# Swapped q and k rows by VectorE's shuffle instead of a second projection, with thirteen tasks of the mix bank laid anew

## The chip, the cores and the metric

One NeuronCore of one Trainium2 chip runs the whole program. The metric is device time in microseconds (us) of one execution; three executions of the kernel before have a median of 373.65 us. Its engines are TensorE (PE: matmuls; PEld: its weight loads), VectorE (DVE), ScalarE (ACT), GpSimd (POOL) and SyncE (SP), each working through its own instructions in order and waiting for the others on semaphores.

## What is computed

A transformer block on 2 x 1024 tokens of width 128, in fp32: attention with 16 heads of width 8, layer norm, a gated feed-forward part with four hidden tiles of 128, layer norm. Of the attention, the part that the change touches is the norm of q and k and the rotation of each half of a head by the other:

```python
half = D // 2
def rot(x):
    x1, x2 = (x[..., :half], x[..., half:])
    return jnp.concatenate([-x2, x1], axis=-1)
...
q, k = _rmsnorm(q, q_scale), _rmsnorm(k, k_scale)     # mean of squares over the 8 of a head
q, k = q * cos + rot(q) * sin, k * cos + rot(k) * sin
...
attn = jax.nn.softmax(q @ k.T, axis=-1)                # after q is scaled by HEAD_DIM ** -0.5
out = (attn @ v) @ w_proj + b_proj
```

## The kernel before

**Layout.** q and k are held transposed: a partition is a feature (8 in a row belong to one head), the free axis holds tokens. The tokens go in four chunks of 512. A chunk of queries is handled in 32 steps: 4 groups of 4 heads, and for each group 8 tiles of 128 keys. A step on TensorE is two pairs of logits (L508, each pair 128 keys by 2 heads by 512 queries into one of three two-bank PSUM tiles) and then the values of the step before (L522, four matmuls of 9 columns each, one a head, which are added up over 8 steps in the O bank, bank 6). ScalarE takes the exponential of each pair (L886, 128x1024), 64 in a chunk, numbered u = 0 to 63. The logits of a pair can be written only when the exponential that last used the PSUM tile has ended, three pairs before.

**The turn of a group.** After 8 steps VectorE moves the O bank to SBUF and turns it (turn_o, L1052), divides by the sums (L1058, L1060), and signals o_copied. The values of the first step of the next group overwrite the O bank, so TensorE waits there (in `values`: if kt == 0, for o_copied) with everything queued behind, the logits that ScalarE takes next among it.

**The mix bank.** Bank 7 serves all that is not attention proper, one task at a time, in a fixed order; each task's TensorE part waits until the one before is read out (mix_free). In the first chunk these tasks prepare q and k of the later token tiles. There are five such blocks (LATE, n = 0 to 4: q of tile 1, k and q of tiles 2 and 3). In the kernel before a block takes three tasks: "proj" (one 128x512 matmul by the weights), "swap" (the same by weights whose columns are swapped within each head, QS or KS of wq) and "var" (the squares by a matrix of means). Two tasks project v of tiles 2 and 3 here ("v"; one more, of tile 1, comes first), and a last one ("flag") tells whether the ternary weights' low parts are all zero. TASK_SLOTS says at which half step TensorE issues each: slot 2s stands between the logits and the values of step s, slot 2s + 1 behind those values. SQUARE_PAIRS and RINV_PAIRS say behind which exponential ScalarE does a block's square (L870, from PSUM) and its Ln and Exp (L877, L879: 1 over the root of the mean).

**VectorE in the first chunk** runs a hand-written list (first_chunk, from L1229): late_products (bank by cosine, waits for the square), late_swap (bank by sine), late_sum, late_rows (by the inverse root, L1202, then the two parts for the store, L1002 and L1004), the turns, and beside these the splits of the weights in a high and a low part (split_weights, L1219 and L1220), the addition of the bias to x (L1247) and four reductions for the flag (largest_low, L1223), whose result (L1274, w_split) the "flag" task takes. VectorE then writes the flags, and TensorE and the others read them (lo_flag) before the loop over chunks 1 to 3 begins. ScalarE loads another table between (L907). GpSimd issues the stores of the parts and the weight loads; SyncE fetches each group's rows.

Of the kernel before, what the change touches and what calls it, by code (L numbers as in the profile page):

```python
# [34 lines left out]
LOGIT_BOUND = 60.0  # L35


MIX_FIRST = 19
MIX_CHUNK = 20

CHAIN_CHUNK = 29
# [39 lines left out]
TASKS = (("v", 1), ("proj", 0), ("swap", 0), ("var", 0),  # L81
         ("proj", 1), ("swap", 1), ("var", 1),
         ("proj", 2), ("swap", 2), ("var", 2), ("v", 2),
         ("proj", 3), ("swap", 3), ("var", 3),
         ("proj", 4), ("swap", 4), ("var", 4), ("v", 3), ("flag", 0))
TASK_SLOTS = (5, 10, 18, 22, 23, 26, 30, 31, 34, 38, 40, 42, 46, 48, 50, 54, 56, 59, 62)
V_PAIR = 7
SQUARE_PAIRS = (11, 23, 31, 43, 51)
RINV_PAIRS = (22, 30, 38, 49, 57)


def tiles_in_turn(swaps):
# [27 lines left out]
def build(nc, x_t, x_n, w_qkv, cols, scale_rows, bias, w_proj, w1, w2, h1, h2, w3, tables, means, eye, out):  # L120
    ctx = ExitStack()
    with ctx:
# [347 lines left out]
        def _(pe):  # L470
# [130 lines left out]
            def first_task(n):  # L601

                kind, i = TASKS[n]
                bank = mix(0)
                if n == 0:
                    pe.wait_ge(rot_done, 8)
                if kind == "flag":
                    pe.wait_ge(w_split, 1)
                    mm = pe.matmul(bank[0:1, 0:1], ve[:, 0:1], ones_c[:], start=True, stop=True)
                elif kind == "v":  # L610
                    mm = project_v(bank, i)
                elif kind == "var":
                    pe.wait_ge(late_sq, i + 1)
                    mm = variance(bank, late_sets[i % 2][0])
                else:
                    t, of = LATE[i]
                    pe.wait_ge(in_x[t], 16)
                    mm = proj(of + (QS if kind == "swap" else 0), bank, t)
                mm.then_inc(mix_ready, 1)

            def keep_warm(count, bank=MIX_BANK):
# [194 lines left out]
        def _(act):  # L816
# [47 lines left out]
                act.nop().then_inc(mix_free, 1)  # L864

            def late_square(n):
                act.wait_ge(mix_ready, TASKS.index(("proj", n)) + 1)
                if n >= 2:
                    act.wait_ge(parts_done, PARTS * (n + 2))
                nc.scalar.activation(late_sets[n % 2][0], ps[:, MIX_BANK, :], ACT.Square).then_inc(late_sq, 1)  # L870

            def late_inverse_root(n):

# [65 lines left out]
        def _(dve):  # L939
# [289 lines left out]
            def first_chunk():  # L1229
# [15 lines left out]
                late_products(1)
                dve.wait_ge(in_res, 64)
                link(nc.vector.tensor_tensor(xb[:], xb[:], bias_b[:, None, :].to_broadcast([P, NCH * TILES, P]), ALU.add), 0)  # L1247
                late_swap(1)
                late_sum(0)
                late_rows(0)  # L1250
# [3 lines left out]
                late_swap(2)
                late_sum(1)
                late_rows(1)
                dve.wait_ge(h1_taken, 1)
                largest_low(0, H1, HM * HID)
# [16 lines left out]
                late_rows(3)
                late_sum(4)
                late_rows(4)
                late_v(3)
# [173 lines left out]
```

## Time and profile before

| | |
|---|---|
| three executions | 373.52, 373.65, 376.35 us (median 373.65) |
| profiled execution, its own time | 374.06 us |
| its span, first to last instruction | 372.0 us |
| mean granted TensorE clock | 0.986 of 2.4 GHz |
| TensorE, ScalarE, VectorE busy | 92%, 82%, 60% of the span |

The span leaves 2.06 us of the profiled execution outside it. Times in rows are microseconds from the span's start unless marked ns. A timeline row joins neighbouring instructions of one line: it gives the start, the length of the whole and the number joined; idle time in front of it and what ended that stand in brackets. TensorE's records count two passes for each fp32 matmul, so one step's values are x8, a projection x2. Busy TensorE is not TensorE at its peak, since matmul ends are modelled and overlap. Waits named for a releaser are inferred.

### The profile page before, as it was taken

The page shows a single profiled execution, that of the slowest core. Times are in us where ns is not written, and L with a number is a line of the kernel's source. Part 1 is how long each engine was busy: PE and PEld are TensorE (multiplying, and loading weights), DVE is VectorE, ACT ScalarE, POOL GpSimd, SP SyncE. Part 2 cuts the span into 40 slices and gives each one's busy share as a digit, 9 for nine tenths or more (in the row PEclk, how much of TensorE's full clock was granted, in tenths as well). Part 3 has the DMA queues.
Part 4 walks back from the last instruction along what each step waited for, and adds up shares of the span by engine and source line. Part 5 has one row for each costly group of instructions (what it writes and reads, how often), then busy time and mean ns, then how long its engine had stood idle before and what let it go on. Part 6 is the DMA issues. An engine that isn't in the chain of part 4 may idle for free.

```text
span 372.0 us, 6282 instructions
## 1 busy us (share of the span) xinstructions
PE 341.7 (92%) x2096; PEld 137.3 (37%) x2101; DVE 221.8 (60%) x468; ACT 305.7 (82%) x353; POOL 29.8 (8%) x43
## 2 busy tenths in 40 slices
PE   8898999998999989999999899999999899999980
PEld 4422223222332444443232544433224544435850
DVE  3996988775457625464467363545576253667753
ACT  3689999899999889789999897989998897854330
POOL 3032111103100000001100000011000000011001
PEclk9989999999999999999999999999999999999996
DMA  7829545326212110201110200203021100000001
GB/s 217 299 104 320 170 160 182 146 90 237 94 34 76 48 56 2 71 32 68 60 65 36 92 9 10 90 0 102 30 97 36 64 0 0 0 29 2 0 0 33
DMA packets 12741, 29.42 MB, mean 79 GB/s; under 512 B 1056, under 2 KB 5040, under 8 KB 12720
## 3 DMA queue, kind: packets, MB, share of 16 engines
q1 hardware_dynamic: 8896, 16.75, 13.3%
q0 software_dynamic: 3392, 12.07, 9.1%
q10 hardware_dynamic: 432, 0.33, 0.4%
q8 instruction: 12, 0.20, 0.3%
q14 instruction: 9, 0.07, 0.1%
HBM read 17.64 MB, written 9.44 MB: 73 GB/s over the span
## 4 chain that ended last, share of the span: by engine, by line
PE 68%; ACT 12%; DVE 10%; issue 6%; DMA 1%; POOL 1%; POOLq 0%; ACTq 0%; DVEq 0%
PE ps L522 25%; PE ps L569 15%; PE ps L508 13%; ACT probs L886 10%; PE ps L688 4%; PE ps L559 4%; DVE ffn L1115 2%; PE ps L472 2%; PE ps L623 2%; DMA srow<-in_scale_rows 1%; PE ps L722 1%; PE ps L539 1%; DVE ffn L1112 1%; PE ps L484 1%; DVE ffn L1129 1%
## 5 line engine op out<-in xcount | busy, mean ns | idle before, releaser
L886 ACT ACTIVATE probs<-ps 128x1024 f32<-128x1024 f32 x256 | 242.8, 1035 | 24.8 <-PE ps L508 24.1
L522 PE MATMUL ps<-probs,va 128*9 128x512 f32 x896 | 112.6, 594 | 3.7 <-ACT probs L886 2.8
L508 PE MATMUL ps<-qa,ka 32*128 32x512 f32 x512 | 77.7, 497 | 6.6 <-ACT probs L886 5.6
L508 PEld LDWEIGHTS ps<-qa,ka 32*128 32x128 f32 x512 | 31.9, 183 | 104.1 <-ACT probs L886 57.4
L1115 DVE TENSOR_SCALAR ffn<-ps,col 128x512 f32<-128x512 f32 x36 | 27.0, 751 | 55.0 <-PE ps L569 50.9
L569 PE MATMUL ps<-g_hi,w_hi 128*128 128x512 f32 x108 | 45.5, 421 | 1.6 <-DVE ffn L1115 1.2
L569 PE MATMUL ps<-g_lo,w_hi 128*128 128x512 f32 x108 | 42.4, 393 | 0.0
L522 PEld LDWEIGHTS ps<-probs,va 128*9 128x9 f32 x896 | 15.8, 89 | 48.9 <-issue 27.6
L1090 DVE TENSOR_TENSOR g_lo<-ffn,g_hi 128x512 fp32r<-128x512 f32 x36 | 24.9, 692 | 1.2
L569 PEld LDWEIGHTS ps<-g_hi,w_hi 128*128 128x128 f32 x108 | 20.2, 187 | 14.5 <-DVE g_lo L1090 4.0
L450 POOL TENSOR_TENSOR rs<-ve,mhalf 128x4 f32<-128x4 f32 x6 | 6.1, 1022 | 228.1 <-DVE ve L1078 228.1
L569 PEld LDWEIGHTS ps<-g_lo,w_hi 128*128 128x128 f32 x108 | 20.3, 188 | 3.4
L522 PE MATMUL ps<-probs,v_all 128*9 128x512 f32 x128 | 17.0, 602 | 1.2 <-ACT probs L886 1.2
L1089 DVE CAST g_hi<-ffn 128x512 fp32r<-128x512 f32 x36 | 15.2, 423 | 4.5 <-ACT ffn L897 3.4
L1052 DVE STREAM_TRANSPOSE o_tok<-ps 128x512 f32<-128x512 f32 x15 | 10.7, 715 | 12.0 <-PE ps L522 12.0
L1112 DVE SCALAR_TENSOR_TENSOR ffn<-ps,col,ffn 128x512 f32<-128x512 f32 x12 | 9.0, 751 | 11.7 <-PE ps L559 11.7
L472 PE MATMUL ps<-xT,wq 128*128 128x512 f32 x28 | 15.1, 633 | 0.1
L897 ACT ACTIVATE ffn<-ffn 128x512 f32<-128x512 f32 (+1 forms) x18 | 12.9, 765 | 2.1 <-DVEq L1119 2.1
L559 PE MATMUL ps<-x_hi,w_hi 128*128 128x512 f32 x24 | 11.9, 496 | 2.9 <-DVE ffn L1115 2.2
L969 DVE SCALAR_TENSOR_TENSOR ffn<-ps,col,rope 128x512 f32<-128x512 f32 x13 | 9.7, 749 | 6.7 <-ACT ffn L870 3.7
L623 PE MATMUL ps<-warm 128*128 128x512 bf16 x48 | 12.8, 393 | 1.0 <-issue 1.0
L930 ACT ACTIVATE ffn<-ps,col 128x512 f32<-128x512 f32 x8 | 4.8, 689 | 9.4 <-PE ps L688 9.4
(133 smaller groups left out, 329.1 us busy)
## 6 DMA issues: line engine op xcount, KB each, us to landing
ka<-k_scr SPq DMA_DIRECT2D x14, 512.0 KB
k_scr<-parts POOLq DMA_DIRECT2D x8, 512.0 KB, 4.2
q_scr<-parts POOLq DMA_DIRECT2D x8, 512.0 KB, 4.8
qa<-q_scr SPq DMA_DIRECT2D x14, 256.0 KB
va<-v_all SPq DMA_DIRECT2D x14, 144.0 KB
ffn<-in_h POOLq DMA_DIRECT2D x1, 1024.0 KB, 9.1
h_raw<-in_h POOLq DMA_DIRECT2D x1, 1024.0 KB, 7.2
xT<-in_x_t SPq DMA_DIRECT2D x3, 256.0 KB, 6.1
```

The lines of the kernel that those rows point to most:

```text
L472: return pe.matmul(bank, wq[:, W_AT[i]:W_AT[i] + P], xT[:, t * CH:(t + 1) * CH], start=True, stop=True)
L508: mm = pe.matmul(s_tile(u)[:, i, :], ka[rows, slot, kt * P:(kt + 1) * P], qa[rows, slot, :], start=True, stop=not shifted)
L522: mm = pe.matmul(ps[32 * h:32 * h + VW, O_BANK, :], v, probs[:, step % 4, h, :], start=(kt == 0), stop=(kt == KT - 1))
L559: mm = pe.matmul(bank, a, x, start=(j == 0), stop=(j == len(todo) - 1))
L569: mm = pe.matmul(bank, w, x, start=(k == 0 and i == 0), stop=(k == HM - 1 and i == len(todo) - 1))
L623: pe.matmul(ps[:, bank, :], warm[:, 0:P], warm[:], start=True, stop=True)
L688: mm = pe.matmul(ps[:, bank0 + m, :], a, (g_hi, g_lo)[part][:, k, :], start=(k == 0 and part == 0 and i == 0), stop=(k == HM - 1 and part ...
L886: nc.scalar.activation(probs[:, step % 4, 2 * pair:2 * pair + 2, :], s_tile(u), ACT.Exp).then_inc(exp_done, 1)
L897: nc.scalar.activation(act_o[:, cols], pre_a[:, cols], ACT.Gelu).then_inc(act_done, 1)
L1089: link(nc.vector.tensor_copy(hi, src), cb)
L1090: return nc.vector.tensor_tensor(lo, src, hi.bitcast(F32), ALU.subtract)
L1115: ins = nc.vector.tensor_scalar(a, mix_bank, col[:, c0 + m:c0 + m + 1], None, ALU.mult)
```

## The change

- The five "swap" tasks go, and with them five projections by the swapped weights. The mix bank has 14 tasks in the first chunk instead of 19.
- In their place late_products first copies the bank to SBUF with the rows of each head turned by half (stream_shuffle on VectorE, by the list HALF_TURN), signals that copy (late_raw), and then multiplies the bank by the cosine. Both no longer wait for a square.
- ScalarE squares the shuffled copy in SBUF instead of the bank. The order of a head's eight rows is another, their sum is the same.
- late_turn takes the place of late_swap: it waits for the square, and multiplies the shuffled copy by the sine, in place.
- The slots of all tasks but the first and the last are new, and so are the places of ScalarE's squares and roots. VectorE's list is in another order.

```diff
-TASK_SLOTS = (5, 10, 18, 22, 23, 26, 30, 31, 34, 38, 40, 42, 46, 48, 50, 54, 56, 59, 62)
+TASK_SLOTS = (5, 12, 18, 21, 26, 30, 34, 36, 39, 44, 47, 52, 56, 62)
...
-SQUARE_PAIRS = (11, 23, 31, 43, 51)
-RINV_PAIRS = (22, 30, 38, 49, 57)
+SQUARE_PAIRS = (15, 23, 32, 41, 49)
+RINV_PAIRS = (19, 27, 35, 45, 53)
+HALF_TURN = [m // HD * HD + (m + HD // 2) % HD for m in range(32)]
...
             def late_square(n):
-                act.wait_ge(mix_ready, TASKS.index(("proj", n)) + 1)
-                if n >= 2:
-                    act.wait_ge(parts_done, PARTS * (n + 2))
-                nc.scalar.activation(late_sets[n % 2][0], ps[:, MIX_BANK, :], ACT.Square).then_inc(late_sq, 1)
+                act.wait_ge(late_raw, n + 1)
+                nc.scalar.activation(late_sets[n % 2][0], late_sets[n % 2][2], ACT.Square).then_inc(late_sq, 1)
...
             def late_products(n):
-                h = late_sets[n % 2][1]
-                mixed(0)
+                h, rot = late_sets[n % 2][1:]
+                k = mixed(0)
+                use[0] += 1
+                t, of = LATE[n]
+                nc.vector.stream_shuffle(rot, mix_bank, HALF_TURN).then_inc(late_raw, 1)
+                turned_by(mix_bank, of, t, h).then_inc(mix_free, 1)
+                dve.wait_ge(mix_free, k + 1)
+
+            def late_turn(n):
+
+                rot = late_sets[n % 2][2]
                 t, of = LATE[n]
                 dve.wait_ge(late_sq, n + 1)
-                turned_by(mix_bank, of, t, h).then_inc(mix_free, 1)
-
-            def late_swap(n):
-
-                t, of = LATE[n]
-                k = mixed(0)
-                use[0] += 1
-                turned_by(mix_bank, of + QS, t, late_sets[n % 2][2]).then_inc(mix_free, 1)
-                dve.wait_ge(mix_free, k + 1)
+                link(turned_by(rot, of + QS, t, rot), 0)
```

The order on each engine is shown at three places. The line numbers after the change are lower by 1 to 3 up to VectorE's list: L507, L521, L471, L483 are the logits, values, projection and means of before's L508, L522, L472, L484.

First TensorE, from the values of step 13 to those of step 16, the first of group 2, which wait for the second turn. Before (v_all is read for groups 0 and 1, va from group 2 on):

```order
L522 MATMUL ps<-probs,v_all 9x512 x4
L508 MATMUL ps<-qa,ka 128x512 x4
L484 MATMUL ps<-ffn,mean 128x512
L522 MATMUL ps<-probs,v_all 9x512 x4
L472 MATMUL ps<-xT,wq 128x512
L508 MATMUL ps<-qa,ka 128x512 x4
L522 MATMUL ps<-probs,v_all 9x512 x4
L508 MATMUL ps<-qa,ka 128x512 x4
L472 MATMUL ps<-xT,wq 128x512
L522 MATMUL ps<-probs,va 9x512 x4
```

After, the same stretch:

```order
L521 MATMUL ps<-probs,v_all 9x512 x4
L507 MATMUL ps<-qa,ka 128x512 x4
L471 MATMUL ps<-xT,wq 128x512
L521 MATMUL ps<-probs,v_all 9x512 x4
L507 MATMUL ps<-qa,ka 128x512 x4
L521 MATMUL ps<-probs,v_all 9x512 x4
L507 MATMUL ps<-qa,ka 128x512 x4
L483 MATMUL ps<-ffn,mean 128x512
L521 MATMUL ps<-probs,va 9x512 x4
```

Before, three tasks lie in this stretch (block 1's means, block 2's projection and swap), and the swap is the last ahead of the values of step 16. After, there are two: block 2's projection, a slot earlier than it was, and block 2's means, which now stand last. Block 1's means lie further ahead (slot 26, where it was 30).

Then VectorE around the same turn (L1052 before, L1049 after). Before:

```order
L1219 CAST w_hi<-h_raw 128x1024
L1220 TENSOR_TENSOR w_lo<-h_raw,w_hi 128x1024
L969 SCALAR_TENSOR_TENSOR ffn<-ps,col,rope 128x512
L1052 STREAM_TRANSPOSE o_tok<-ps 128x512
L1058 RECIPROCAL rden<-o_tok 128x16
L1060 TENSOR_TENSOR attn<-o_tok,rden 128x16x8
L969 SCALAR_TENSOR_TENSOR ffn<-ps,col,rope 128x512
L1195 TENSOR_TENSOR ffn<-ffn 128x512
L1202 TENSOR_TENSOR ffn<-ffn 128x512
L1002 CAST parts<-ffn 128x512
L1004 TENSOR_TENSOR parts<-ffn,parts 128x512
```

After:

```order
L1179 STREAM_SHUFFLE ffn<-ps 128x512
L966 SCALAR_TENSOR_TENSOR ffn<-ps,col,rope 128x512
L1200 TENSOR_TENSOR ffn<-ffn 128x512
L999 CAST parts<-ffn 128x512
L1001 TENSOR_TENSOR parts<-ffn,parts 128x512
L1217 CAST w_hi<-h_raw 128x1024
L1218 TENSOR_TENSOR w_lo<-h_raw,w_hi 128x1024
L1049 STREAM_TRANSPOSE o_tok<-ps 128x512
L1055 RECIPROCAL rden<-o_tok 128x16
L1057 TENSOR_TENSOR attn<-o_tok,rden 128x16x8
L966 SCALAR_TENSOR_TENSOR ffn<-ffn,col,rope 128x512
L1193 TENSOR_TENSOR ffn<-ffn 128x512
```

Before, one product stood between the split of the second hidden weight (L1220 on h_raw) and the turn, and that product was block 2's own. Now block 2's shuffle and product come first, then block 1's inverse root and its two parts (L1200, L999, L1001), then the split, and then the turn. The third turn has block 4's shuffle and product and block 3's rows in front of it in the same way.

Last the end of VectorE's list. Before:

```order
L1223 TENSOR_REDUCE stats<-w_lo 128x1 x2
L1274 TENSOR_REDUCE ve<-stats 128x1
L1202 TENSOR_TENSOR ffn<-ffn 128x512
L1002 CAST parts<-ffn 128x512
L1004 TENSOR_TENSOR parts<-ffn,parts 128x512
L1195 TENSOR_TENSOR ffn<-ffn 128x512
L1202 TENSOR_TENSOR ffn<-ffn 128x512
L1002 CAST parts<-ffn 128x512
L1004 TENSOR_TENSOR parts<-ffn,parts 128x512
L1208 COPY v_all<-ps 128x4x4x8 x4
L1280 TENSOR_SCALAR flags<-ps 1x1
```

After:

```order
L1218 TENSOR_TENSOR w_lo<-ffn,w_hi 128x512
L1221 TENSOR_REDUCE stats<-w_lo 128x1
L1200 TENSOR_TENSOR ffn<-ffn 128x512
L999 CAST parts<-ffn 128x512
L1001 TENSOR_TENSOR parts<-ffn,parts 128x512
L1206 COPY v_all<-ps 128x4x4x8 x4
L1221 TENSOR_REDUCE stats<-w_lo 128x1
L1274 TENSOR_TENSOR xb<-xb,bias_b 128x2048
L1221 TENSOR_REDUCE stats<-w_lo 128x1
L1276 TENSOR_REDUCE ve<-stats 128x1
L1278 TENSOR_SCALAR flags<-ps 1x1
L1279 SCALAR_TENSOR_TENSOR flags<-flags 1x1
```

The addition of the bias (xb) came in the middle of the list before and now stands next to the end, between the last reductions. The reduction on which the flag task waits (writes ve) stood before the last two blocks' rows and the copy of v, and is now behind all of them.

## Rows read from the trace of the kernel before

**Rows 1.** The page: busy time, share and instructions of each engine.
```profile
PE 341.7 (92%) x2096; PEld 137.3 (37%) x2101; DVE 221.8 (60%) x468; ACT 305.7 (82%) x353; POOL 29.8 (8%) x43
```

**Rows 2.** Busy time by stretch: the first chunk from pair 8 on.
```profile
core 0: us, PE busy (x) PEld busy (x) DVE busy (x) ACT busy (x) POOL busy (x), PEclk, DMA share, GB/s
27.00:90.10 63.10, 60.02 (x376) 16.48 (x372) 50.12 (x79) 60.54 (x71) 10.99 (x16) 1.00 0.55 190
```

**Rows 3.** Groups by line, 27 to 90.2 us: busy and mean, idle before.
```profile
line engine op names shapes xcount | busy us, mean ns | idle before us <-releasers
L886 ACT ACTIVATE probs<-ps 128x1024 f32<-128x1024 f32 x56 | 53.0, 1042 | 2.5 <-PE ps L508 2.4 <-ACT v_all L836 0.2
...
L969 DVE SCALAR_TENSOR_TENSOR ffn<-ps,col,rope 128x512 f32<-128x512 f32 x10 | 7.5, 751 | 6.7 <-ACT ffn L870 3.7 <-PE ps L472 2.2 <-issue 0.8
...
L877 ACT ACTIVATE ffn<-ps,eps_c 128x512 f32<-128x512 f32 x5 | 3.5, 698 | 0.0
...
L879 ACT ACTIVATE ffn<-ffn 128x512 f32<-128x512 f32 x5 | 3.2, 631 | 0.2
L870 ACT ACTIVATE ffn<-ps 128x512 f32<-128x512 f32 x5 | 3.0, 608 | 0.0
```

**Rows 4.** Timeline, ScalarE: start, length, and in brackets idle before it.
```profile
27.05 3.77 ACT L886 ACTIVATE probs<-ps 128x1024 f32<-128x1024 f32 x4 [0.17 <-ACT v_all L836]
...
39.02 2.85 ACT L886 ACTIVATE probs<-ps 128x1024 f32<-128x1024 f32 x3 [0.37 <-PE ps L508]
...
48.47 2.85 ACT L886 ACTIVATE probs<-ps 128x1024 f32<-128x1024 f32 x3 [0.31 <-PE ps L508]
...
67.82 3.77 ACT L886 ACTIVATE probs<-ps 128x1024 f32<-128x1024 f32 x4 [0.73 <-PE ps L508]
...
90.11 1.28 ACT L907 ACT_TABLE_LOAD   x1
91.41 7.44 ACT L886 ACTIVATE probs<-ps 128x1024 f32<-128x1024 f32 x8
```

**Rows 5.** Timeline, TensorE, where group 2 begins and at the chunk's end.
```profile
55.36 1.12 PE L472 MATMUL ps<-xT,wq 128*128 128x512 f32 x2
56.41 1.05 PE L522 MATMUL ps<-probs,va 128*9 128x512 f32 x8
...
88.32 1.05 PE L522 MATMUL ps<-probs,va 128*9 128x512 f32 x8 [0.17 <-ACT probs L886]
90.61 0.63 PE L508 MATMUL ps<-qa,ka 32*128 32x512 f32 x4 [1.25 <-ACT probs L886]
```

**Rows 6.** Timeline, VectorE: a shuffle, and the work around the second turn.
```profile
27.65 0.72 DVE L992 STREAM_SHUFFLE r<-ffn 128x512 f32<-128x512 f32 x1
...
42.19 0.69 DVE L1219 CAST w_hi<-h_raw 128x1024 fp32r<-128x1024 f32 x1
...
45.27 2.28 DVE L1247 TENSOR_TENSOR xb<-xb,bias_b 128x2048 f32<-128x2048 f32 x1
...
50.90 0.85 DVE L1219 CAST w_hi<-h_raw 128x1024 fp32r<-128x1024 f32 x1
51.78 1.23 DVE L1220 TENSOR_TENSOR w_lo<-h_raw,w_hi 128x1024 fp32r<-128x1024 f32 x1
...
54.76 0.71 DVE L1052 STREAM_TRANSPOSE o_tok<-ps 128x512 f32<-128x512 f32 x1
...
58.10 0.69 DVE L1202 TENSOR_TENSOR ffn<-ffn 128x512 f32<-128x512 f32 x1
58.83 0.43 DVE L1002 CAST parts<-ffn 128x512 fp32r<-128x512 f32 x1
...
80.81 1.81 DVE L1223 TENSOR_REDUCE stats<-w_lo 128x1 f32<-128x1024 f32 x2
...
87.03 0.88 DVE L1208 COPY v_all<-ps 128x128 f32<-128x128 f32 x4
...
88.55 0.14 DVE L1282 CAST flags_i<-flags 1x1 int32<-1x1 f32 x1
```

More of the change, by code:

```diff
@@ L35 @@
 LOGIT_BOUND = 60.0
-MIX_FIRST = 19
+MIX_FIRST = 14
 MIX_CHUNK = 20
@@ L80 @@
 LATE = ((1, Q), (2, K), (2, Q), (3, K), (3, Q))
[L81 to L85, printed above, removed]
-TASK_SLOTS = (5, 10, 18, 22, 23, 26, 30, 31, 34, 38, 40, 42, 46, 48, 50, 54, 56, 59, 62)
+TASKS = (("v", 1), ("proj", 0), ("var", 0), ("proj", 1), ("var", 1), ("proj", 2), ("var", 2), ("v", 2),
+         ("proj", 3), ("var", 3), ("proj", 4), ("var", 4), ("v", 3), ("flag", 0))
+TASK_SLOTS = (5, 12, 18, 21, 26, 30, 34, 36, 39, 44, 47, 52, 56, 62)
 V_PAIR = 7
-SQUARE_PAIRS = (11, 23, 31, 43, 51)
-RINV_PAIRS = (22, 30, 38, 49, 57)
+SQUARE_PAIRS = (15, 23, 32, 41, 49)
+RINV_PAIRS = (19, 27, 35, 45, 53)
+HALF_TURN = [m // HD * HD + (m + HD // 2) % HD for m in range(32)]
 def tiles_in_turn(swaps):
@@ L228, in build @@
         sq_done = sem("sq_done")
+        late_raw = sem("late_half_turned")
         late_sq = sem("late_square_done")
@@ L617, in first_task @@
                     pe.wait_ge(in_x[t], 16)
-                    mm = proj(of + (QS if kind == "swap" else 0), bank, t)
+                    mm = proj(of, bank, t)
                 mm.then_inc(mix_ready, 1)
@@ L1237, in first_chunk @@
                 late_products(0)
-                turn_group(0)
-                late_swap(0)
                 dve.wait_ge(in_h1, 16)
                 split_half(h1_raw, H1, 0)
+                turn_group(0)
+                late_turn(0)
+                late_sum(0)
+                late_products(1)
                 split_half(h1_raw, H1, 1).then_inc(h1_taken, 1)
+                late_rows(0)
+                late_turn(1)
+                late_sum(1)
                 dve.wait_ge(in_h2, 16)
                 split_half(h2_raw, H2, 0)
[L1245 to L1250, printed above, removed]
+                late_products(2)
+                late_rows(1)
                 link(split_half(h2_raw, H2, 1), 0)
-                late_products(2)
                 turn_group(1)
[L1254 to L1258, printed above, removed]
+                late_turn(2)
                 late_sum(2)
@@ L1262, in first_chunk @@
                 late_products(3)
-                largest_low(1, H2, HM * HID)
-                late_swap(3)
+                dve.wait_ge(h1_taken, 1)
+                largest_low(0, H1, HM * HID)
+                late_turn(3)
+                late_sum(3)
                 dve.wait_ge(in_w123, 48)
                 split_weights(w_raw[:, 0:2 * HID], W1, 2 * HID)
+                late_products(4)
+                late_rows(3)
                 turn_group(2)
+                late_turn(4)
+                late_sum(4)
                 link(split_weights(w_raw[:, 2 * HID:2 * HID + HM * P], W3, HM * P), 0)
-                late_products(4)
-                late_sum(3)
-                late_swap(4)
+                largest_low(1, H2, HM * HID)
+                late_rows(4)
+                late_v(3)
                 largest_low(2, W1, 2 * HID)
+                dve.wait_ge(in_res, 64)
+                nc.vector.tensor_tensor(xb[:], xb[:], bias_b[:, None, :].to_broadcast([P, NCH * TILES, P]), ALU.add)
                 link(largest_low(3, W3, HM * P), 0)
                 nc.vector.tensor_reduce(ve[:, 0:1], w_max[:, 0:4], AX.X, ALU.max).then_inc(w_split, 1)
[L1275 to L1278, printed above, removed]
                 mixed(0)
```

## The prediction

> **What bounds the kernel now.** The page's first part comes first: TensorE is busy 92% of the span, ScalarE 82%, VectorE 60% [rows 1]. The change touches only the first chunk, so the next view is the busy time of that stretch alone. From 27.0 us, where pair 8 begins, to 90.1, TensorE has 60.0 and ScalarE 60.5 of 63.1 us at a granted clock of 1.00; VectorE has 50.1 [rows 2]. So two engines are nearly full, and the question is which ends each wait. The groups by line answer: ahead of its 56 exponentials ScalarE idled 2.5 us in all, 2.4 of it for TensorE's logits [rows 3]. The timeline shows these as short pieces, 0.37, 0.31 and 0.73, and three more of 0.31 to 0.32, while between them the exponentials run one behind the other [rows 4]. ScalarE sets the pace of this chunk and TensorE's tasks push it off by 2.35 us. That is also the most that a perfect rearrangement can give, for ScalarE keeps all its work. VectorE's 6.7 us of idle time ahead of its products [rows 3] cost nothing by themselves.
>
> **What goes and what comes.** (a) Five swaps go: 5 x 1.06 = 5.3 us of TensorE (1.12 by the row, of which about 0.06 lies under the next matmul: 55.36 to 56.41) [rows 5]. TensorE is not first in the chain, so this can give back only parts of the 2.35. (b) Five shuffles are added on VectorE. No row has one that reads PSUM. Those that read SBUF take 0.72 us, the transposition of the same 128x512 out of PSUM takes 0.71, a plain cast 0.43, and the four copies of v out of PSUM 0.88 together [rows 6]. I take 0.72 as the nearest in kind, with 0.43 and 0.88 as bounds. (c) The five sine products now read SBUF, and stay at the 0.75 us that these products have on average [rows 3]. (d) ScalarE's square reads SBUF. From PSUM it took 608 ns; an activation of the same size from SBUF, the exponential of L879, 631, and the slowest of that size, L877, 698 [rows 3]. I take 0.02 each, 0.1 in all; nothing and 0.45 are the bounds.
>
> By the Trainium skill, VectorE: DVE Perf Modes, section on the TRN2 errata, a ScalarE instruction has a fixed part of 224 cycles out of SBUF and of 172 out of PSUM; as an estimate from that page this speaks against (d) with 43 ns each, 0.2 us in all. The trace agrees in sign, at 23 ns, and by that rule the forecast would be 0.1 us later.
>
> **The walk.** What is left is order: when does each engine reach its waits? I follow the changed program with the pitches of these rows. An exponential takes 0.92 to 0.93 (8 in 7.44, the last 1.02 long), I use 0.925, and ends 1.02 after its start [rows 4]; Ln with Exp takes 1.27 and a square about 0.48, both their lengths of 0.70, 0.63 and 0.61 less the overlap of some 0.1 with what follows. On TensorE values take 0.98, a step's logits 0.44 when nothing holds them (they are ready 0.5 after the start), a task 1.06, less the same overlap [rows 5]. A VectorE instruction that the next one waits for takes its length and 0.03.
>
> *Pair 14.* Pair 8 starts at 27.05 [rows 4], so ScalarE wants pair 14 at 27.05 + 6 x 0.925 = 32.6; the square that stood behind pair 11 and gave TensorE half a microsecond now comes behind pair 15. TensorE starts the values of step 4 when exponential 9 ends (29.0). Behind them come logits, block 0's projection (slot 12), values and the logits of step 7: 29.0 + 0.98 + 0.44 + 1.06 + 0.98 + 0.5 = 33.0. Idle 0.4.
>
> *Pairs 20 and 28.* No swap stands ahead of them any more; the 0.37 and 0.31 go. Up to pair 28 ScalarE does one Ln and Exp more than before (behind pair 27, not 30), so it starts pair 28 at 48.47 + 1.27 - 0.68 + 0.40 = 49.5.
>
> *Pair 32.* TensorE's second logits of step 15 wait for exponential 28 (50.5), the projection of block 2 follows at 50.9 and is ready at 52.05; values to 53.0, logits ready at 53.5. ScalarE wants them at 49.5 + 4 x 0.925 = 53.2. Idle 0.35.
>
> *The second turn.* VectorE has waited for this projection. From 52.1 it does shuffle 0.75, product 0.78, block 1's inverse root 0.72, cast 0.46, subtraction 0.61 (0.69 less an overlap of 0.08), then the split's cast, 0.72 if it is not stretched, and subtraction, 1.26 [rows 3, 6]. It starts the transposition at 57.4 and ends it at 58.1. Before, it started it at 54.76, right behind one product [rows 6]. TensorE wants the O bank as soon as block 2's means are done. The square behind pair 32 ends at 55.0, the means at 56.1. So the values of step 16 wait 56.1 to 58.1, where before they went without a wait at 56.41 [rows 5]. This stall of 2.0 us is the main step of the forecast. ScalarE has pairs up to 35 and Ln and Exp, until 59.0. TensorE brings pair 36 at 58.1 + 0.98 + 0.53 = 59.6: idle 0.6. Then the v task (slot 36) stands ahead of pair 38 (59.5 + 1.09 + 0.98 + 0.53 = 62.1, wanted at 61.5: 0.6) and block 3's projection (slot 39) with values ahead of pair 40 (64.6, wanted 64.0: 0.6). Sum 1.8.
>
> *The third turn.* Exponential 45 ends at 64.6 + 5 x 0.925 + 0.48 + 1.02 = 70.7, then values to 71.7, block 4's projection to 72.85. VectorE: shuffle, product, block 3's root, cast and subtraction, 3.3 us, so the transposition runs from 76.2 to 76.9. TensorE wants the O bank at 75.3. ScalarE, with its square behind pair 49, wants pair 52 at 77.9, and gets it at 76.95 + 0.98 + 0.53 = 78.5: idle 0.6. The catching up, with the tasks of slots 52 and 56, costs about 0.35 more, an estimate from the 0.31 to 0.37 that single tasks cost before [rows 4].
>
> *Sum.* Idle after: 0.4 + 0.35 + 1.8 + 0.6 + 0.35 = 3.5 us, where it was 2.35. With 0.1 for the squares that is +1.25. The profiled execution took 374.06 us, so 375.3; it lay 0.4 above the median of 373.65, by which it is 374.9. I give **375.0 us**, +1.2 on either within rounding.
>
> *The end of the chunk.* VectorE goes on from 76.9: the rest of the turn 0.6, product and sum 1.5, split 1.1, the reduction of 2048 elements 2.2 (as the bias addition of that length, 2.28 with overlap), root and parts 1.8, then, from 84.2 when v is there, copies 0.95, reductions 1.1 + 0.5, the bias 2.2, the last reduction 0.2 [rows 6]: w_split at 89.2. TensorE is then at the flag task, 89.0. So the bias, which cost nothing in the middle of the list, has almost no cover left here. Flags are written at 90.1. TensorE ends its values at 90.4, needs 1.3 us for load and branch (88.32 + 0.98 to 90.61) and has logits at 92.3 [rows 5]. ScalarE ends at about 91.2 and its table at 92.5 [rows 4]. This just fits, by 0.2 us, as it did before (91.1 to 91.41). I cost it at nothing; every tenth that VectorE loses beyond these 0.2 costs a tenth. The later chunks' code stays and starts later by the same 1.2. GpSimd's three weight loads wait for the first hidden weight's second half, which is now split behind block 1's product, about 2 us later than it was. Behind them GpSimd holds the stores of blocks 0 to 4. Block 0's parts come earlier in VectorE's list than before, and the first use of any of these is the next chunk's, so I cost this at nothing.
>
> **Rivals.**
> *The turns don't bind (faster).* If VectorE ends the second turn by 59.0 - 0.98 - 0.53 = 57.4, 0.7 earlier than walked, pair 36 loses nothing; shuffles at their lower bound (0.3 earlier) with a projection 0.4 earlier would do it. With both turns free there remain 0.4, 0.35, some 0.85 at pairs 38 and 40 where tasks crowd, and 0.4: 2.0 against 2.35, so 0.35 faster, 373.3. If all idle goes too, 371.3 (373.65 - 2.35). For it speaks the 5.3 us taken off TensorE; against it, that in these rows VectorE had one product ahead of the turn and now has seven instructions. Chance 0.25.
> *The end comes late (slower still).* If VectorE is later than walked by 1 us, from a shuffle at 0.88 (0.8 in all) and casts that stretch beside GpSimd's stores, as 0.85 for 0.69 in these rows [rows 6], then the turns and w_split each pass on most of it: 0.3 + 0.3 at the turns and 0.7 at the end, +2.5, so 376.2. Against it: VectorE still idles about 2 us ahead of blocks 2 and 4, which takes up what came before. Chance 0.13.
> *Nothing seen (within 0.4 of before).* The squares are cheap and one turn binds, the other not: 3.5 - 1.0 = 2.5 of idle, 373.8. Chance 0.12.
> My forecast, both turns bind, +0.5 to +2: 0.50.
>
> **Numbers.** The range runs from the free turns to the late end with its bounds: 373.1 to 376.6. It leaves out the case of no idle at all and a late end past 3 us. A measurement of this kernel can tell about 1%, 3.7 us, from no change. The most that can be gained is 2.35, so faster by that much is next to excluded, 0.01; slower by 3.7 needs the late end at 1.5 times its price, 0.04; within 1% has 0.95.
>
> **What would show it.** In the changed profile ScalarE's idle ahead of its exponentials in this chunk should sum to about 3.5 us, with gaps of 0.5 to 0.7 at pairs 36, 38, 40 and 52 (about 59, 62, 64 and 78 us). The values' wait for the transposition should appear as about 2 us twice; the second transposition should start near 57.4. The table load should come near 91.3, where it came at 90.11. Shuffles should read 0.72, squares 0.63. The forecast is wrong if the transpositions start before 56.5, if the table load comes before 90.1, or if more than 0.3 us pass between the table's end and the next exponential.

## The result, and the profile after

The changed kernel takes **378.9 us** (median of 4 runs, 376.3 to 379.9) where the kernel before took 373.7 beside it: ratio 1.0127, 95% interval 1.0095 to 1.0158. It is slower by 5.2 us; that is 3.9 above the forecast of 375.0 and outside its range of 373.1 to 376.6, and a loss of over 3.7 us had been given a chance of 0.04. In this document an execution more than 1.5% above the fastest of its kernel is left out of the ratios, but not of the medians and ranges.

The profiled execution took 379.01 us. ScalarE's timeline, with the idle time ahead of a row in brackets, shows where the time went:

```profile
33.05 1.94 ACT L883 ACTIVATE probs<-ps 128x1024 f32<-128x1024 f32 x2 [0.47 <-PE ps L507]
35.34 0.63 ACT L867 ACTIVATE ffn<-ffn 128x512 f32<-128x512 f32 x1 [0.35 <-DVE ffn L1179]
...
53.99 1.02 ACT L883 ACTIVATE probs<-ps 128x1024 f32<-128x1024 f32 x1 [0.31 <-PE ps L507]
...
61.48 1.94 ACT L883 ACTIVATE probs<-ps 128x1024 f32<-128x1024 f32 x2 [1.96 <-PE ps L507]
65.75 1.94 ACT L883 ACTIVATE probs<-ps 128x1024 f32<-128x1024 f32 x2 [2.34 <-PE ps L507]
68.22 1.02 ACT L883 ACTIVATE probs<-ps 128x1024 f32<-128x1024 f32 x1 [0.52 <-PE ps L507]
...
82.25 1.94 ACT L883 ACTIVATE probs<-ps 128x1024 f32<-128x1024 f32 x2 [0.68 <-PE ps L507]
...
86.36 3.77 ACT L883 ACTIVATE probs<-ps 128x1024 f32<-128x1024 f32 x4 [0.90 <-PE ps L507]
90.48 1.02 ACT L883 ACTIVATE probs<-ps 128x1024 f32<-128x1024 f32 x1 [0.34 <-PE ps L507]
...
96.10 1.28 ACT L904 ACT_TABLE_LOAD   x1
97.39 1.02 ACT L883 ACTIVATE probs<-ps 128x1024 f32<-128x1024 f32 x1
```

The table load comes at 96.10, where it came at 90.11 [rows 4]. From pair 8 to there it is 6.1 us more, so the loss is made in this one chunk. The gaps lie where the walk put them (pairs 14, 32, 36, 38, 40, 52 and the catching up, 0.90 and 0.34), and one more, 0.35, stands ahead of the first square. Those at 36, 38 and the catching up are more than three times their forecast size. The groups by line say the same: 7.7 us of idle ahead of the exponentials against 2.5 [rows 3].

```profile
L883 ACT ACTIVATE probs<-ps 128x1024 f32<-128x1024 f32 x56 | 53.1, 1030 | 7.7 <-PE ps L507 7.5 <-ACT v_all L835 0.2
L1179 DVE STREAM_SHUFFLE ffn<-ps 128x512 f32<-128x512 f32 x5 | 3.7, 737 | 0.0
L867 ACT ACTIVATE ffn<-ffn 128x512 f32<-128x512 f32 x5 | 3.2, 634 | 0.4 <-DVE ffn L1179 0.4
```

What made them large stands in TensorE's timeline around the second and the third turn:

```profile
55.68 1.10 PE L483 MATMUL ps<-ffn,mean 128*128 128x512 f32 x2
58.81 1.90 PE L521 MATMUL ps<-probs,va 128*9 128x512 f32 x8 [2.04 <-DVE o_tok L1049]
...
61.37 2.08 PE L478 MATMUL ps<-wq,xT 128*128 128x128 f32 x8
63.38 1.90 PE L521 MATMUL ps<-probs,va 128*9 128x512 f32 x8
...
80.73 1.04 PE L521 MATMUL ps<-probs,va 128*9 128x512 f32 x8 [1.80 <-ACT probs L883]
...
82.14 1.93 PE L483 MATMUL ps<-ffn,mean 128*128 128x512 f32 x2
84.01 1.88 PE L521 MATMUL ps<-probs,va 128*9 128x512 f32 x8
```

The stall of 2.04 us is the one that was forecast, 0.7 us later. But the values behind it take 1.90 us, not 1.05 [rows 5], and the v task 2.08: TensorE works at half speed until 65.3. Behind the stall of 1.80 (put down to the exponential; VectorE's transposition, from 79.88 to 80.59, ended last) values and logits still take their usual time, and from about 82.3 to 85.7 the same happens. The windows carry the reason in the third column from the end, the granted clock:

```profile
core 0: us, PE busy (x) PEld busy (x) DVE busy (x) ACT busy (x) POOL busy (x), PEclk, DMA share, GB/s
27.00:58.00 31.00, 26.70 (x164) 6.86 (x160) 26.16 (x44) 29.80 (x35) 7.97 (x12) 1.00 0.67 232
58.00:66.00 8.00, 7.19 (x36) 2.67 (x40) 4.89 (x12) 3.66 (x6) 0.00 (x0) 0.57 0.42 160
...
80.00:88.00 8.00, 7.27 (x39) 1.65 (x40) 7.69 (x11) 6.39 (x8) 1.39 (x3) 0.79 0.54 195
```

In single microseconds from 59 to 65 it is 0.50, the lower of the two levels, 1.2 GHz for 2.4. Before, it was 1.00 from pair 8 to the table load [rows 2]. By the Trainium skill, TensorE: Matmul & The Clock Gate, Part 1 on the clock gate, the clock follows how busy the engine has lately been, and one kernel can meet the gate differently from run to run; the rows here agree with both, the second as the two traces of one kernel in experiment 9 show.

VectorE's timeline ahead of the second turn holds the seven instructions of the walk (two of them, block 1's cast and subtraction, 0.43 and 0.69, are not shown) and then the transposition:

```profile
52.59 0.74 DVE L1179 STREAM_SHUFFLE ffn<-ps 128x512 f32<-128x512 f32 x1
53.23 0.74 DVE L966 SCALAR_TENSOR_TENSOR ffn<-ps,col,rope 128x512 f32<-128x512 f32 x1
54.00 0.69 DVE L1200 TENSOR_TENSOR ffn<-ffn 128x512 f32<-128x512 f32 x1
...
55.80 0.86 DVE L1217 CAST w_hi<-h_raw 128x1024 fp32r<-128x1024 f32 x1
56.69 1.22 DVE L1218 TENSOR_TENSOR w_lo<-h_raw,w_hi 128x1024 fp32r<-128x1024 f32 x1
57.95 0.72 DVE L1049 STREAM_TRANSPOSE o_tok<-ps 128x512 f32<-128x512 f32 x1
```

### The profile page after: what moved, and what is told of

Same layout as the page of the kernel before. It is cut to its first block, busy times and chain, and to the rows that moved or that the text cites. A ratio compares the mean times of both kernels' runs of the same rounds, so it can differ in the third digit from the quotient of the medians.

```text
span 376.9 us, 6266 instructions
## 1 busy us (share of the span) xinstructions
PE 341.9 (91%) x2091; PEld 136.4 (36%) x2091; DVE 225.4 (60%) x478; ACT 305.8 (81%) x353; POOL 29.9 (8%) x43
## 4 chain that ended last, share of the span: by engine, by line
PE 63%; DVE 17%; ACT 10%; issue 6%; DMA 2%; POOL 1%; DVEq 0%; POOLq 0%; ACTq 0%
PE ps L521 24%; PE ps L568 15%; PE ps L507 11%; ACT probs L883 8%; PE ps L558 4%; PE ps L687 4%; DVE ffn L1112 2%; PE ps L622 2%; DMA srow<-in_scale_rows 2%; DVE r L989 1%; PE ps L721 1%; DVE ffn L966 1%; PE ps L538 1%; PE ps L471 1%; PE ps L478 1%
## 5 line engine op out<-in xcount | busy, mean ns | idle before, releaser
L521 PE MATMUL ps<-probs,va 128*9 128x512 f32 x896 | 115.2, 606 | 8.1 <-ACT probs L883 5.2
L507 PE MATMUL ps<-qa,ka 32*128 32x512 f32 x512 | 78.6, 497 | 7.3 <-ACT probs L883 6.1
L507 PEld LDWEIGHTS ps<-qa,ka 32*128 32x128 f32 x512 | 31.9, 182 | 108.5 <-ACT probs L883 56.6
L568 PE MATMUL ps<-g_hi,w_hi 128*128 128x512 f32 x108 | 45.4, 421 | 1.7 <-DVE ffn L1112 1.2
L568 PE MATMUL ps<-g_lo,w_hi 128*128 128x512 f32 x108 | 42.5, 393 | 0.0
L521 PEld LDWEIGHTS ps<-probs,va 128*9 128x9 f32 x896 | 15.8, 89 | 51.5 <-issue 25.8
L521 PE MATMUL ps<-probs,v_all 128*9 128x512 f32 x128 | 16.7, 595 | 2.4 <-ACT probs L883 2.1
L1049 DVE STREAM_TRANSPOSE o_tok<-ps 128x512 f32<-128x512 f32 x15 | 10.7, 714 | 9.0 <-PE ps L521 9.0
L687 PE MATMUL ps<-g_lo,w_hi 128*128 128x512 f32 x36 | 11.6, 403 | 0.6 <-DVE g_lo L1366 0.6
L687 PE MATMUL ps<-g_hi,w_hi 128*128 128x512 f32 x36 | 11.5, 400 | 0.0
```

Of the source, the lines that this page charges most:

```text
L507: mm = pe.matmul(s_tile(u)[:, i, :], ka[rows, slot, kt * P:(kt + 1) * P], qa[rows, slot, :], start=True, stop=not shifted)
L521: mm = pe.matmul(ps[32 * h:32 * h + VW, O_BANK, :], v, probs[:, step % 4, h, :], start=(kt == 0), stop=(kt == KT - 1))
L568: mm = pe.matmul(bank, w, x, start=(k == 0 and i == 0), stop=(k == HM - 1 and i == len(todo) - 1))
L687: mm = pe.matmul(ps[:, bank0 + m, :], a, (g_hi, g_lo)[part][:, k, :], start=(k == 0 and part == 0 and i == 0), stop=(k == HM - 1 and part ...
L1049: nc.vector.transpose(o_tok[:, g % 2, :], ps[:, O_BANK, :]).then_inc(o_copied, 1)
```

## The experiments

Each is told by its time and by the stretch from pair 8's start to the table load, which leaves out how late pair 8 comes (26.3 to 29.8 us in the twelve traces): **63.06 us before, 69.13 after**. The kernel before had medians of 373.4 us beside experiments 1, 2, 3 and 7, 373.5 beside 4, 5, 6 and 8, and 373.6 beside 9. The expectations name kernels by labels: e1, e2 and e3 are experiments 1, 2 and 3, e8 is 4, e6 is 5, e5 is 6, e4 is 7, e7 is 8, and e9 and e10 are 9.

**1. The turns ahead of the work that delayed them.** In VectorE's list of the changed kernel:

```
 late_products(2)
+turn_group(1)
 late_rows(1)
 link(split_half(h2_raw, H2, 1), 0)
-turn_group(1)
...
 late_products(4)
+turn_group(2)
 late_rows(3)
-turn_group(2)
```

> The changed kernel with its second and third turn moved ahead of the rows that stood in front of them. Theory A (TensorE's stall for the turns of 2.0 and 1.8 us costs twice: as a wait, and by the granted clock at half, 1.2 GHz, for the 4 to 6 us behind it): both stalls go, the clock stays at 1.00 from 27 us to the chunk's end, and of the 5.2 us of loss some 4 come back: 374 to 375 us. What is left is the end of the list, where the flag waits for VectorE. Theory B (the waits alone, the clock's fall has another cause): the stalls go, the half-clock stretches stay, about 376.5 us. Theory C (the shuffles' work on VectorE is the loss, wherever the turns stand): 377.5 us or more.

Measured: 375.8 us (375.5 to 377.1), ratio 1.0056 (1.0039 to 1.0073), and a stretch of 62.97: both stalls and both falls of the clock are gone, and the chunk is as long as before. So the turns made the whole loss up to the table load. But 2.3 us stay in the time, which is above the expected 374 to 375, and they lie just behind the table load, where ScalarE waits 1.36, 0.73 and 0.38 us. First VectorE's timeline at the end of its list, then TensorE's, then the window:

```profile
87.23 2.28 DVE L1274 TENSOR_TENSOR xb<-xb,bias_b 128x2048 f32<-128x2048 f32 x1
89.43 0.68 DVE L1221 TENSOR_REDUCE stats<-w_lo 128x1 f32<-128x512 f32 x1
90.14 0.16 DVE L1276 TENSOR_REDUCE ve<-stats 128x1 f32<-128x4 f32 x1
```

```profile
90.45 0.16 PE L608 MATMUL ps<-ones_c,ve 128*1 128x1 f32 x1 [1.75 <-DVE ve L1276]
```

```profile
88.00:97.00 9.00, 6.60 (x42) 1.32 (x38) 4.21 (x10) 6.89 (x8) 0.00 (x0) 0.66 0.19 65
```

TensorE waits 1.75 us at the flag task for the last reduction, behind the bias addition, and the clock falls again. The 2.3 us hold the waiting and the fall together. In the changed kernel the turns' delay had covered it (0.50 us at the flag, nothing ahead of the next exponential at 97.39).

**2. The same stalls, filled.** Nine and eight matmuls of zeros are put ahead of the values of steps 16 and 24, into a tile that the next logits overwrite; the output is untouched.

```
+FILL = {17: 9, 25: 8}
...
+if step in FILL:
+    u = 2 * (step + 1)
+    pe.wait_ge(exp_done, max(v for v in range(u) if TILE_OF[v] == TILE_OF[u]) + 1)
+    keep_warm(FILL[step], 2 * TILE_OF[u])
```

> The changed kernel, but ahead of the values of steps 16 and 24 TensorE runs 9 and 8 matmuls of 128x512 bf16 on zeros into the PSUM tile that the next logits overwrite. The stalls for the turns stay as long as they are, only TensorE is busy in them. Theory A: the granted clock stays 1.00 through 58 to 66 and 82 to 86 us, ScalarE's idle ahead of its exponentials falls from 7.7 us to about 4.5, and the time is 375.5 to 376. Theory B (waits alone, clock from elsewhere): the half-clock stretches stay and the time with them, 378 to 379 us.

Measured: 375.4 us (375.3 to 376.0), ratio 1.0054 (1.0037 to 1.0071), stretch 65.50. At the second turn VectorE is as late and the values wait as long (TensorE, then the window, then ScalarE):

```profile
56.08 1.89 PE L623 MATMUL ps<-warm 128*128 128x512 bf16 x8
58.06 1.05 PE L522 MATMUL ps<-probs,va 128*9 128x512 f32 x8
```

```profile
58.00:66.00 8.00, 7.87 (x56) 2.53 (x56) 6.47 (x15) 6.07 (x8) 1.34 (x2) 1.00 0.49 188
```

```profile
59.58 1.94 ACT L888 ACTIVATE probs<-ps 128x1024 f32<-128x1024 f32 x2 [0.81 <-PE ps L508]
62.08 1.94 ACT L888 ACTIVATE probs<-ps 128x1024 f32<-128x1024 f32 x2 [0.56 <-PE ps L508]
64.55 1.94 ACT L888 ACTIVATE probs<-ps 128x1024 f32<-128x1024 f32 x2 [0.53 <-PE ps L508]
```

With the fallen clock go 3.5 us of time (378.9 to 375.4; against the kernel before beside each, the loss falls from 5.2 to 2.0 us) and 3.6 of the stretch. The three gaps are now 0.81, 0.56 and 0.53, where the walk had 0.6 each. By the gaps the first fall cost 2.9 us (4.8 to 1.9 at pairs 36 to 40).

At the third turn the filler itself ran too long (TensorE, VectorE, ScalarE):

```profile
75.84 1.67 PE L623 MATMUL ps<-warm 128*128 128x512 bf16 x7 [0.57 <-ACT probs L888]
77.45 1.05 PE L522 MATMUL ps<-probs,va 128*9 128x512 f32 x8
...
76.22 0.71 DVE L1054 STREAM_TRANSPOSE o_tok<-ps 128x512 f32<-128x512 f32 x1
...
78.96 1.94 ACT L888 ACTIVATE probs<-ps 128x1024 f32<-128x1024 f32 x2 [1.05 <-PE ps L508]
```

The turn ends at 76.93 and the values start only at 77.45, some 0.5 behind it, where at the second turn they start 0.14 behind it (57.92 to 58.06). So of the gap of 1.05 at pair 52 about 0.4 is the filler's, and of what is left, +2.4 in the stretch and 2.0 in the time, about 2.0 of the stretch is the waiting itself.

**3. A late turn in the kernel before.** No shuffle, no other slot; only `turn_group(1)` moved behind `late_swap(2)`.

> The kernel before, no shuffle in it, with one edit: the second turn stands behind block 2's sine product instead of ahead of it. No work is added. By the rows of before the transposition then runs from about 57.4 to 58.1 us, while TensorE wants the O bank at 56.4: a stall of 1.7 us. Theory A: behind it the granted clock falls to 0.50 for some 4 us, and the kernel loses 2.5 to 3.5 us, 376.2 to 377.2. Theory B: no fall of the clock, a loss of 0.5 to 1.2 us, 374.2 to 374.9.

Measured: 376.8 us (374.8 to 379.6, 10 runs), ratio 1.0098 (1.0065 to 1.0132). The order alone, with no shuffle in the kernel, makes a loss of this kind. The ten times fall into two groups: four at 374.8 to 375.8 us with a granted clock of 0.987 to 0.993 over the whole run, four at 378.8 to 379.6 with 0.975 to 0.979, and two between (376.4 and 377.1, 0.981 and 0.982). The profiled one was of the first group (375.8):

```profile
58.76 1.04 PE L522 MATMUL ps<-probs,va 128*9 128x512 f32 x8 [1.69 <-DVE o_tok L1052]
```

```profile
60.28 2.85 ACT L886 ACTIVATE probs<-ps 128x1024 f32<-128x1024 f32 x3 [2.07 <-PE ps L508]
```

Behind 1.69 us of stall the values take 1.04: here the clock did not fall, ScalarE lost 1.8 us once (stretch 64.82), and that is all. So the median lies where theory A had it, and the trace shows theory B's mechanism, at a higher price than its 0.5 to 1.2. One stall costs about its length; the long executions take 3.8 us more. That the clock fell behind the stall in those is an inference from their run's clock: none of them was traced, and a run's clock does not tell where it fell.

**4. The same with the stall filled** (seven matmuls of zeros ahead of the values of step 16, as in 2).

> The kernel of e3 (before, second turn behind block 2's sine product) with 7 matmuls of 128x512 bf16 on zeros ahead of the values of step 16, into the PSUM tile that the next logits overwrite. The runs of e3 fell in two groups: 374.8 to 375.8 us with a mean granted clock of 0.987 to 0.993, and 376.4 to 379.6 with 0.975 to 0.982. Theory A (in the second group the clock fell behind the stall of 1.7 us): with TensorE busy in the stall only the first group is left, 374.8 to 375.8 in every execution. Theory B (the second group has another cause): both groups stay.

Measured: 375.9 us (374.7 to 378.0, 5 runs), ratio 1.0074 (1.0039 to 1.0109), stretch 64.82, equal to experiment 3's without the filler. Theory A wanted every execution at 374.8 to 375.8. Three are there within 0.1; one took 376.5 at a run's clock of 0.980, and one 378.0 at 0.942, lower than any run of experiment 3, and no trace shows why. Five runs against ten do not show that the filler removes the long executions.

**5. Only the second turn early** (the first part of experiment 1's diff).

> The changed kernel with only the second turn moved ahead of block 1's rows; the third turn stays late (a stall of 1.8 us in the changed kernel) and so does the end of the list. It prices the two stalls apart. Theory A: no half-clock stretch at 58 to 66 us, the one behind the third turn stays in the executions in which it comes, 375.5 to 377.5, between e1 and the changed kernel. If the second stall were all of the loss: 373.5 to 374.5.

Measured: 375.6 us (374.1 to 378.3, 10 runs), ratio 1.0065 (1.0036 to 1.0094), stretch 65.26. The third turn alone costs 2.3 us in the profiled execution, TensorE stalling 1.80, with the clock at 0.84 from 78 to 88 us:

```profile
76.42 1.05 PE L521 MATMUL ps<-probs,va 128*9 128x512 f32 x8 [1.80 <-ACT probs L883]
...
77.83 2.08 PE L483 MATMUL ps<-ffn,mean 128*128 128x512 f32 x2
```

The second turn is then worth the other 3.9 us of the stretch (69.13 to 65.26). In time experiment 1 (375.8) has no gain over this one: what its earlier third turn gives back, the wait at the end of the list takes.

**6. The turns early, and the bias addition out of the list's end.** Experiment 1, and the bias addition moved ahead of `late_rows(0)`.

> The kernel of e1 (changed kernel, second and third turn ahead of the rows) with one edit more: the addition of the bias stands ahead of block 0's rows instead of between the last reductions. e1 left one stall of TensorE, 1.75 us for the flag's reduction, and a granted clock of 0.66 from 88 to 97 us behind it. Theory A: the reduction comes 2.2 us earlier, this stall goes, the clock stays at 1.00 through the chunk, and the time falls from e1's 375.6 by 2 to 2.8 us, to 372.9 to 373.6, that of the kernel before. Theory C (the shuffles' load on VectorE costs by itself): it stays at 375 or more.

Measured: 373.7 us (373.0 to 376.7), ratio 1.0017 (0.9997 to 1.0038), stretch 62.93. The flag task has no wait. So turns and bias account for the whole loss, within the interval (which leaves room for 1.4 us): three places in VectorE's list. What the change itself adds and takes away, shuffles and squares against swaps, comes to nothing that these runs can tell. The profiled execution was the longest, 376.7, with the stretch of a short one: its pair 8 came only at 29.79.

**7. The changed kernel laid anew.** Slots (5, 10, 20, 22, 26, 28, 30, 33, 40, 42, 46, 52, 54, 62), squares behind pairs 16, 24, 28, 41, 47, roots behind 20, 26, 31, 43, 52. VectorE's list from block 1's product on, cut to its order:

```
 late_products(1), late_rows(0), split h2 (0)
 late_turn(1), late_products(2), late_sum(1), largest_low(0), late_turn(2)
 turn_group(1)
 split W1, late_v(2), split h2 (1), late_rows(1), late_sum(2)
 late_products(3), split W3, largest_low(2), late_turn(3), late_rows(2), late_sum(3)
 late_products(4), turn_group(2), late_turn(4), late_rows(3)
 largest_low(1), largest_low(3), late_v(3), late_sum(4), bias, late_rows(4), reduction
```

> Shuffles as in the change, with slots (5, 10, 20, 22, 26, 28, 30, 33, 40, 42, 46, 52, 54, 62), squares behind pairs 16, 24, 28, 41, 47, roots behind 20, 26, 31, 43, 52, and VectorE's list in an order in which each turn is reached before TensorE wants the O bank, and the bias addition ends before the last block's rows. Theory A, with the walk by the pitches of the rows: ScalarE's idle in the chunk falls to 0.4 to 1.1 us against 2.35 before, no fall of the clock, 1.5 to 2 us faster than before: 371.7 to 372.2. Theory C (the shuffles themselves overload VectorE): no arrangement gets below before, 374 us or more.

Measured: **372.4 us** (372.0 to 373.5, 8 runs), ratio 0.9977 (0.9963 to 0.999): about 1.0 us faster than before, 6.4 faster than the changed kernel. The stretch is 61.03, ScalarE idles 0.3 for logits and 0.4 for a shuffle (the 0.5 in the first row below holds 0.2 ahead of pair 8):

```profile
L883 ACT ACTIVATE probs<-ps 128x1024 f32<-128x1024 f32 x56 | 52.5, 1047 | 0.5 <-PE ps L507 0.3 <-ACT v_all L835 0.2
L867 ACT ACTIVATE ffn<-ffn 128x512 f32<-128x512 f32 x5 | 3.2, 645 | 0.4 <-DVE ffn L1179 0.4
```

VectorE now waits for TensorE ahead of the second turn, and not the other way round:

```profile
54.98 0.72 DVE L1049 STREAM_TRANSPOSE o_tok<-ps 128x512 f32<-128x512 f32 x1 [0.46 <-PE ps L521]
```

**8. The same with each shuffle made twice.**

```
+link(nc.vector.stream_shuffle(rot, mix_bank, HALF_TURN), 0)
 nc.vector.stream_shuffle(rot, mix_bank, HALF_TURN).then_inc(late_raw, 1)
```

> The kernel laid anew (e4) with each of the five shuffles made twice, one behind the other: 5 x 0.77 = 3.8 us more on VectorE, each ahead of the square. It doubles the work that the change adds. Theory A (the work counts only through what comes late): squares come 0.5 to 0.8 us late for three blocks, some 1.7 us in all, and more if VectorE begins its list late: 374.2 to 375.5 against e4's 372.4. If VectorE's load didn't count at all: 372.4. If it counted in full: 376.2.

Measured: 375.3 us (373.2 to 379.6, 10 runs), ratio 1.0044 (1.002 to 1.0067), stretch 63.36. Five more shuffles are 3.9 us of VectorE (the second starts 0.77 to 0.78 behind the first) and cost 2.3 us of the stretch. Three of ScalarE's squares now wait for VectorE, 0.80, 1.14 and 0.56 us:

```profile
51.55 0.63 ACT L867 ACTIVATE ffn<-ffn 128x512 f32<-128x512 f32 x1 [0.80 <-DVE ffn L1180]
```

So with the idle time gone VectorE's time is not free either: it works 54.2 of the 61 us from 27 to 88.

**9. The kernel before laid anew, with its swaps.** Same aims as in 7, for 19 tasks: slots (5, 12, 18, 20, 22, 26, 28, 31, 34, 36, 38, 40, 44, 48, 49, 52, 56, 59, 62), squares behind 13, 23, 31, 41, 49, roots behind 21, 29, 36, 48, 57, the second turn right behind block 2's product and the third ahead of block 4's, the bias addition behind `late_swap(1)`.

> The kernel before, with its swaps and all 19 tasks, and its slots, squares, roots and VectorE's list laid anew with the same aims as in the rearranged changed kernel (its turns in time, the bias addition early). It tells whether that kernel's gain of 1.0 us (stretch from pair 8 to the table load 61.03 us against 63.06 before) is owed to the shuffles. Theory 1 (the swaps' 5.3 us of TensorE are what has to go): ScalarE keeps most of its 2.35 us of idle time, since TensorE with 60.0 us of work in 63.1 has nearly none to give; walked the stretch is 62.4 to 62.7 us, so 372.8 to 373.2 where before has 373.4. Theory 2 (the arrangement alone gives it): idle below 0.9 us, stretch 61 to 61.5, 372.2 to 372.6. The granted clock should be 1.00 in both, with no wait of TensorE over 1 us.

> The rearranged changed kernel once more, on the same chip as the rearranged kernel before: 372.4 us, stretch 61.0, two gaps of 0.3 to 0.4. If theory 1 holds the two differ by 1.0 to 1.6 us in the stretch; if theory 2 holds, by under 0.5.

Measured, on one chip: the kernel before laid anew 372.8 us (371.9 to 378.8, 12 runs), ratio 1.0002 (0.9975 to 1.0028); the changed one laid anew 372.1 (370.6 to 375.5, 12 runs), ratio 0.9966 (0.9939 to 0.9994). The stretches are 63.15 and 61.02. ScalarE's groups of the kernel before laid anew:

```profile
L886 ACT ACTIVATE probs<-ps 128x1024 f32<-128x1024 f32 x55 | 52.0, 1033 | 2.2 <-PE ps L508 2.0 <-ACT v_all L836 0.2
```

With the swaps in, ScalarE's idle time stays, 2.2 us here and 0.3 more ahead of a root: a new order moved it and took nothing away. In the stretch, the gain of 2.1 us needs the swaps gone, as theory 1 has it, and was more than expected, since here the expected 0.4 to 0.7 from order alone did not come. In the times it is not shown: 8 of these 12 runs lie at 371.9 to 373.2, near those of the changed kernel laid anew, and the two intervals overlap. That another order of this list gives nothing is not shown, only that this one didn't.

The repeated kernel also showed the clock once more. In the first of its traces TensorE waits 1.18 us for the exponentials at the table load and goes on at full speed; in the second, with the same program, it waits 1.36:

```profile
89.00 0.91 PE L507 MATMUL ps<-qa,ka 32*128 32x512 f32 x4 [1.36 <-ACT probs L883]
89.84 1.90 PE L521 MATMUL ps<-probs,va 128*9 128x512 f32 x8
```

and the clock from 89 to 92 is 0.51, 0.50 and 0.50; ScalarE loses 0.24 and 0.73 behind the table load.

## Why the prediction was wrong

**The step that failed** is the sentence "This stall of 2.0 us is the main step of the forecast" and all that follows it, at pairs 36 to 40 and in the catching up behind the third turn: TensorE's stall was found, placed and sized rightly, and then priced as a wait alone, with values at 0.98 and a task at 1.09 behind it. The granted clock of 1.00 was read from [rows 2] as a property of the stretch, where TensorE had no such wait; behind both new stalls it fell. At 0.50, values, the v task and values again took 1.90, 2.08 and 1.90 us, and pair 36, walked at 59.6 with the turn 0.7 earlier, came at 61.5. Filled, the same stalls cost 3.5 us less. The filled kernel's 375.4 us lies 0.4 from the forecast, but partly by luck: against the kernel before beside it, it lost 2.0 us, not 1.2.

Point by point:
- *ScalarE sets the pace; at most 2.35 us to gain.* Right: experiment 7 took 2.0 of the 2.35 in the stretch.
- *Pairs 14 and 32: 0.4 and 0.35.* 0.47 and 0.31.
- *Block 0's square.* Missed: it waited 0.35 for its shuffle, as VectorE came to it at 34.55, 0.7 behind the end of its q and k work. It was costed at nothing without a look at when VectorE is free there.
- *Second turn: transposition at 57.4, stall 2.0.* 57.95 and 2.04. VectorE was 0.5 late, as block 2's projection was.
- *Pairs 36, 38, 40: 0.6 each.* 1.96, 2.34 and 0.52 at the fallen clock; 0.81, 0.56 and 0.53 without the fall. These terms were right but for the clock.
- *Third turn: 0.6, catching up 0.35.* 0.68 in the changed kernel, where pair 52's logits were written before the clock fell; the fall then made 1.24 of the catching up. Filled, 1.05 and 0.35, with about 0.4 of the 1.05 made by the filler. The turn's 0.6 was right. Experiment 5, where only this turn was late, gives 2.3 us with a fallen clock.
- *Squares 0.1.* They took 634 ns for 608, as 0.63 was forecast, and the next exponential starts 0.52 behind them for 0.48 before: 5 x 0.04 to 0.05, some 0.2. By the Trainium skill, VectorE: DVE Perf Modes, section on the TRN2 errata, it would be 43 ns each, an estimate from its cycles; the trace shows 26.
- *Shuffles 0.72.* 0.74; they took the value of the nearest kind. Right.
- *Sum +1.25.* With the clock held +2.4 in the stretch and +2.0 in the time. The 4.4 us of idle against the forecast 3.5 are 0.45 at the third turn (nearly all the filler's), 0.3 at the square, and 0.15 spread over the rest. Without the filler's share the waiting is some +2.0 in the stretch, 0.8 above the sum.
- *The end of the chunk, fits by 0.2.* In the changed kernel nothing was lost there, but only as ScalarE was 6 us late. With the turns repaired TensorE waited 1.75 us for VectorE's last reduction. The remark that the bias "has almost no cover left here" was right. The price that the rival of the late end put on it had another cause, a slower VectorE: counted from pair 8, the reduction ended at 62.4 us, only 0.3 later than walked (89.2 less 27.05), and it was TensorE that came to the flag task 1.1 earlier than walked (60.8 for 61.95), as the turns no longer held it up.
- *The later chunks start later by the same.* Right: the last but one of ScalarE's rows lags 5.9 us at the end as at the table load; some 1.0 of it returns behind the issue of the last store (371.75 for 365.89 us, with the span's end at 376.9 for 372.0).

## What to carry over

When a change makes TensorE wait in one piece where it was nearly full (2.04 and 1.80 us here), reckon with a halved clock behind the stall, in some executions or in all, and price it by what waits on TensorE then: 2.9 us behind the second turn here, 0.5 to 0.9 behind the third. Look in every in-order list for the items on which that engine waits, and walk to each; here three places in VectorE's list (two turns and a bias addition) decided 5 us, and the added and removed instructions at most 2. A filler of useless matmuls tells the clock's share from the waiting's in one run, if it does not outlast the wait.

## What was not expected of the hardware

- **The clock falls behind a stall, not surely.** Behind TensorE's stalls of 2.04, 1.80, 1.80, 1.75 and 1.36 us it fell to 0.50; behind 1.69 (experiment 3), 1.33 (experiment 4, table load) and 1.18 it did not, nor in experiment 6 behind a wait of 1.75 for a transfer at the table load. In experiment 8 it did not fall behind one of 1.37 either:

```profile
67.22 1.10 PE L483 MATMUL ps<-ffn,mean 128*128 128x512 f32 x2 [1.37 <-ACT ffn L867]
```

Length alone doesn't decide it. In the changed kernel it stayed at 0.50 for some 6.8 us at the second turn and 3.4 at the third, though the engine was busy without a pause. What decides between executions was not tried.
- **It also falls before pair 8, in the kernel before too.** In six of the twelve traces, that of before among them (17.1 to 20.5 us), the clock is 0.50 for some 3 us between 17 and 25, though TensorE's longest wait near there, 1.01 to 1.02, is in all twelve. Experiment 6's trace has a second such stretch from 7.3 us, behind a wait of 1.97 for a transfer, and the latest pair 8. The stretch from pair 8 on leaves this out; a time or a run's clock does not, so falls here may be part of why executions of one kernel differ.
- **One kernel, short and long times.** Kernels with such a stall have runs some 4 to 6 us apart (experiments 3, 5, 8), with a whole run's clock mostly of 0.974 to 0.982 in the long ones and 0.986 to 0.993 in the short ones (376.1 us at 0.985 in experiment 8 is an exception); even the kernel before laid anew has four of 12 at 375.6 to 378.8. Medians of few runs of such a kernel are uncertain by that, the 378.9 of the changed kernel included: one of its four took 376.3 at a clock of 0.987.
